# Joining the first attention's output projection with the normalisation behind it, and three changes of order around DMA queues

## The reference, cut to what matters

```python
n = layernorm(x)                                     # rows of 256
q, k, v = n @ Wq.T, ctx @ Wk.T, ctx @ Wv.T           # layer 0: 32 query heads of 8, 8 key groups
o = softmax(q k^T * 8**-0.5) v
x = x + o @ Wfc.T + bfc                              # the projection, its bias and the sum
x = x + moe_gelu(layernorm(x))                       # layer 0, feed-forward
...                                                  # layers 1 and 2
x = x + ffn_relu2(layernorm(x))                      # layer 2, feed-forward
x = x + attention_l3(layernorm(x), ctx)              # layer 3: 16 heads, keys quantised
x = x + moe_silu(layernorm(x))                       # layer 3: experts' weights are 16 x 512 KB of w1, 8 x 512 KB of w2
```

## Time and profile before

| | |
|---|---|
| median of 3 runs | 1090.81 us (1089.27 to 1090.97) |
| the profiled execution's own time | 1090.98 us |
| its span in the profile | 1089.3 us |
| first attention, first to last of its instructions | 16.2 to 177.7 us |
| its projection and normalisation, to the first instruction behind | 178.0 to 195.6 us |
| ffn_relu2's last DVE instruction, next block's first | 620.6 and 625.6 us |

### The profile page before, as it was taken

How to read it: one execution, slowest core, us unless ns; L and a number is a source line. 1 busy time by engine, 2 the same in 40 slices (tenths; PEclk the granted TensorE clock), 3 DMA queues, 4 the chain that set the end, 5 groups by cost and what they waited for, 6 DMA issues and landing times. The chain is left out here.

```text
span 1089.3 us, 15385 instructions
## 1 busy us (share of the span) xinstructions
PE 931.0 (85%) x5416; PEld 540.0 (50%) x5416; DVE 618.8 (57%) x1290; ACT 528.1 (48%) x797; POOL 257.7 (24%) x304
## 2 busy tenths in 40 slices
PE   5689897999799548889979678888888799999997
PEld 2244444666469415434436543343345565666664
DVE  4667764444534777725456489999995431211214
ACT  3166664322243584577843248899896211222210
POOL 4001010000000000414423236766775050000014
PEclk9689999899899869999979985555555699999999
DMA  3611410100358102576550647878653021111013
GB/s 116 168 34 53 112 37 12 38 1 1 116 60 69 32 0 78 149 181 141 81 202 23 143 150 146 166 131 193 143 101 67 0 78 44 49 44 44 25 34 101
DMA packets 130541, 91.63 MB, mean 84 GB/s; under 512 B 92853, under 2 KB 119775, under 8 KB 128687
## 3 DMA queue, kind: packets, MB, share of 16 engines
q1 hardware_dynamic: 125618, 83.45, 34.0%
q0 software_dynamic: 1536, 4.20, 1.2%
q10 hardware_dynamic: 3312, 3.02, 0.8%
HBM read 56.09 MB, written 15.86 MB: 66 GB/s over the span
## 5 line engine op out<-in xcount | busy, mean ns | idle before, releaser
L2360 ACT ACTIVATE sb_l_E<-PS,sb_l_NB,sb_L3SQS 128x1024 uint8<-128x1024 f32 x128 | 154.5, 1207 | 18.7 <-DVE sb_l_NB L2409 9.2
L2406 DVE TENSOR_REDUCE sb_l_NM<-PS 128x1 f32<-128x1024 f32 x128 | 155.5, 1215 | 1.9 <-PE PS L2307 1.9
L2307 PE MATMUL PS<-sb_l_K,sb_l_Q 128*128 128x512 bf16 x256 | 127.2, 599 | 30.4 <-ACT sb_l_E L2360 19.9
L2251 POOL CAST sb_l_ET<-sb_l_EP 128x1024 bf16<-128x1024 uint8 x127 | 128.1, 1046 | 57.1 <-DMA sb_l_EP<-sb_l_E 52.9
L613 DVE TENSOR_REDUCE sb_negmax<-PS 128x2 f32<-128x512 f32 x128 | 84.1, 690 | 32.0 <-PE PS L463 31.7
L2317 PEld LDWEIGHTS PS<-sb_L3VI,sb_l_ET 128*128 128x128 bf16 x1024 | 55.8, 113 | 68.3 <-issue 49.3
L599 ACT ACTIVATE sb_E<-PS 128x1024 f32<-128x1024 f32 x64 | 65.5, 1024 | 42.6 <-PE PS L526 42.5
L1368 PE MATMUL PS<-sb_L3w,sb_block_xT 128*128 x184 | 82.8, 593 | 0.7 <-issue 0.7
L923 ACT ACTIVATE sb_E<-PS 128x1024 f32<-128x1024 f32 x64 | 65.4, 1024 | 24.9 <-PE PS L830 21.2
L463 PE MATMUL PS<-sb_K,sb_Q 96*128 96x256 bf16 x256 | 54.0, 303 | 15.9 <-ACT sb_negmax_T L573 10.3
L846 POOL MEMSET sb_rms_eps<- 128x1 f32 x1 | 0.1, 100 | 275.5 <-POOLq L180 275.5
(11 more groups left out here) (356 smaller groups left out, 1768.3 us busy)
## 6 DMA issues: line engine op xcount, KB each, us to landing
sb_Q<-q SPq DMA_DIRECT2D x48, 192.0 KB
sb_L3w<-L3w SPq DMA_DIRECT2D x16, 512.0 KB, 7.1
sb_K<-k SPq DMA_DIRECT2D x24, 192.0 KB
sb_W2E<-L3w SPq DMA_DIRECT2D x8, 512.0 KB, 4.3
q<-sb_q_parts SPq DMA_DIRECT2D x12, 256.0 KB, 4.1
xs<-zero_row SPq DMA_DIRECT2D x1, 2944.0 KB, 47.2
sb_block_x<-xs SPq DMA_DIRECT2D x23, 128.0 KB, 2.1
ys<-sb_block_y ACTq DMA_DIRECT2D x23, 128.0 KB, 2.4
```

What stands on the lines that cost most here:

```text
L2251: return eng.tensor_copy(ET[:, u % CRING], EP[:, u // 2 % TRING, :, :, u % 2])
L2307: ins = pe.matmul(core.bank(2 * (n % SRING) + half), Q[:, h % RING, t * P:(t + 1) * P], K[:, h % RING, half * HALF:(half + 1) * HALF], sta ...
L2360: act.activation(E[:, n // 2 % ERING, :, n % 2], S(n), ACT.Exp, bias=NB[:, n:n + 1], scale=scale_of(h, t), accum_out=ZS[:, n:n + 1]).then_ ...
L2406: dve.tensor_reduce(NM[:, n:n + 1], S(n), axis=AX.X, op=ALU.max, negate=True).then_inc(maxed, 1)
```

## The change

- `project_norm` replaces `out_project` and the `layer_norm` behind it: one block, with the order of the last attention's end. The bias is added to tiles 0 to 3 by DVE at the start of its list and to tiles 4 to 7 by POOL; the bias itself is loaded during the attention as one of its prefetches.
- `attention_l0`: slot 0 of Q is written straight from the parts in SBUF, 9 DMAs of 64 KB (send_q), and the stores of the first half follow them. Groups 2 and 3 are loaded after the first and second copy of maxima. The first two copies of maxima are sent by ACT's own queue. The exp table is loaded before. copy_max stands ahead of the exp.
- `ffn_relu2`: the last six w1 loads go to the end of the list that `attention_l3` works off head by head (18 entries instead of 12), and the wait for the stores of k16 moves from the end of the block to just before attention_l3's key loads.

```diff
@@ -250,68 +251,137 @@
...
-def out_project(core, Wo, bias_dram):
...
+def project_norm(core, Wo, BB, weights):
     nc = core.nc
...
+    HN = NT // 2
+    old = core.take_old()
...
+    features = lambda half, c: core.XT[:, c, half * HALF:(half + 1) * HALF]
...
         with nc.Block() as block:
             @block.sync
             def _(sp):
...
+                sp.wait_ge(out_done, NT // 2)
+                for dst, src in weights:
+                    sp.dma_start(dst, src).then_inc(core.weights_in, 16)
+            @block.gpsimd
+            def _(pool):
+                for t in range(HN, NT):
+                    pool.tensor_tensor(core.X[:, t, :], core.X[:, t, :], BB[:, :], ALU.add).then_inc(biased_p, 1)
+                for handle in old:
+                    pool.sem_clear(handle)
             @block.tensor
             def _(pe):
                 for half in range(2):
                     for c in range(NC):
...
+                        for j in range(HN):
+                            ins = pe.transpose(core.PS[:, 2 * half + c, j * P:(j + 1) * P],
+                                               core.XN[:, HN * half + j, c * P:(c + 1) * P], core.identf[:, :])
+                        ins.then_inc(out_turned, 1)
+                for half in range(2):
+                    pe.wait_ge(xt_a, half + 1)
+                    pe.wait_ge(xt_v, half + 1)
+                    for t in range(HN * half, HN * half + HN):
+                        for c in range(NC):
+                            ins = pe.matmul(core.PS[:, 4 + t // 2, (t % 2) * D:(t % 2 + 1) * D],
+                                            core.XT[:, c, t * P:(t + 1) * P], Wo[:, c, :],
+                                            start=(c == 0), stop=(c == NC - 1))
+                        if t % 2:
+                            ins.then_inc(out_done, 1)
+                for half in range(2):
+                    for j in range(HN):
+                        t = HN * half + j
+                        pe.wait_ge(ln_a if t % 2 else ln_v, t // 2 + 1)
+                        for c in range(NC):
                             ins = pe.transpose(core.PS[:, 2 * half + c, j * P:(j + 1) * P],
                                                core.XN[:, t, c * P:(c + 1) * P], core.identf[:, :])
...
+                            if j == HN - 1:
+                                ins.then_inc(ln_turned, 1)
             @block.scalar
             def _(act):
                 act.preload_act_table_set("sqrt_and_others")
                 for half in range(2):
...
+                    act.wait_ge(out_turned, 2 * half + 1)
+                    act.activation(features(half, 0), core.bank(2 * half), ACT.Copy).then_inc(xt_a, 1)
+                for half in range(2):
+                    T = slice(HN * half, HN * half + HN)
+                    act.wait_ge(aggr, HN * (half + 1))
+                    act.activation(SD[:, T], MV[:, T, 1], ACT.Sqrt, bias=core.ln_eps[:, 0:1]).then_inc(std, 1)
+                    act.wait_ge(shift, half + 1)
+                    for t in range(HN * half + 1, HN * half + HN, 2):
+                        act.activation(core.XN[:, t, :], core.X[:, t, :], ACT.Identity, bias=SH[:, t:t + 1],
+                                       scale=RS[:, t:t + 1]).then_inc(ln_a, 1)
+                for half in range(2):
+                    act.wait_ge(ln_turned, 2 * half + 1)
+                    act.activation(features(half, 0), core.bank(2 * half), ACT.Copy)
             @block.vector
             def _(dve):
+                def add_out(pair):
+                    dve.wait_ge(out_done, pair + 1)
+                    dve.tensor_tensor(core.X[:, 2 * pair:2 * pair + 2, :],
+                                      core.PS[:, 4 + pair, :].rearrange("p (t d) -> p t d", d=D),
+                                      core.X[:, 2 * pair:2 * pair + 2, :], ALU.add).then_inc(added, 1)
+                def stats(pair):
+                    dve.wait_ge(added, pair + 1)
+                    for t in (2 * pair, 2 * pair + 1):
+                        core.row_stats(dve, t).then_inc(measured, 1)
+                def mean_var(half):
+                    dve.wait_ge(measured, HN * (half + 1))
+                    for t in range(HN * half, HN * half + HN):
+                        dve.bn_aggr(MV[:, t, :], core.ST[:, t, :]).then_inc(aggr, 1)
+                def normalise(half):
+                    T = slice(HN * half, HN * half + HN)
+                    dve.wait_ge(std, half + 1)
+                    dve.reciprocal(RS[:, T], SD[:, T]).then_inc(rstd, 1)
+                    dve.wait_ge(rstd, half + 1)
+                    dve.scalar_tensor_tensor(out=SH[:, T], in0=MV[:, T, 0], scalar=-1.0, in1=RS[:, T],
+                                             op0=ALU.mult, op1=ALU.mult).then_inc(shift, 1)
+                    for t in range(HN * half, HN * half + HN, 2):
+                        dve.tensor_scalar(core.XN[:, t, :], core.X[:, t, :], MV[:, t, 0:1], RS[:, t:t + 1],
+                                          ALU.subtract, ALU.mult).then_inc(ln_v, 1)
+                for t in range(HN):
+                    dve.tensor_tensor(core.X[:, t, :], core.X[:, t, :], BB[:, :], ALU.add).then_inc(biased_v, 1)
                 for half in range(2):
...
+                    dve.wait_ge(out_turned, 2 * half + 2)
+                    dve.tensor_copy(features(half, 1), core.bank(2 * half + 1)).then_inc(xt_v, 1)
+                dve.wait_ge(biased_v, HN)
+                add_out(0)
+                add_out(1)
+                stats(0)
+                stats(1)
+                mean_var(0)
+                dve.wait_ge(biased_p, HN)
+                add_out(2)
+                normalise(0)
+                add_out(3)
+                stats(2)
+                stats(3)
+                mean_var(1)
+                normalise(1)
+                for half in range(2):
+                    dve.wait_ge(ln_turned, 2 * half + 2)
+                    dve.tensor_copy(features(half, 1), core.bank(2 * half + 1))
...
 def attention_l0(core, Wq, Wk, Wv, VE, q8, k8, ones_dram, scale, prefetch):
@@ -408,6 +478,9 @@
                         load_k(g, r)
                         load_q(g, r)
 
+                def send_q(i, r):
+                    sp.dma_start(Q[PR * r + i:PR * (r + 1):PARTS, 0, :], QP[0:R8 * PER, 0, i, :]).then_inc(q_in[0], 16)
+
                 def load_max(n):
                     g, h = n // 2, n % 2
                     sp.wait_ge(max_out, n + 1)
@@ -422,19 +495,22 @@
                 sp.wait_ge(padded, 1 + RING)
                 sp.dma_start(K[RK:RK + PARTS, :, :].rearrange("p r t -> p (r t)"), ones_dram).then_inc(k_ones, 16)
                 for i, done in enumerate((high, middle, low)):
-                    store_q(0, i, done, stored_q0)
                     sp.wait_ge(stored_k[i], 16)
                     load_k(0, i)
-                sp.wait_ge(stored_q0, 16 * PARTS)
-                for r in range(PARTS):
-                    load_q(0, r)
+                    sp.wait_ge(done, 4)
+                    for r in range(PARTS):
+                        send_q(i, r)
+                for i, done in enumerate((high, middle, low)):
+                    store_q(0, i, done, stored_q0)
                 for i, done in enumerate((high, middle, low)):
                     store_q(1, i, done, stored_q1)
+                sp.wait_ge(stored_q0, 16 * PARTS)
                 load(1)
-                load(2)
-                load(3)
+                for g in range(2, RING):
+                    sp.wait_ge(max_out, g - 1)
+                    load(g)
                 sp.wait_ge(stored_q1, 16 * PARTS)
-                for n in range(HALVES):
+                for n in range(2, HALVES):
                     load_max(n)
                     g = n // 2
                     if n % 2 and g >= 1:
@@ -455,7 +531,7 @@
                 def max_scores(m):
                     g, b, j = m // MAXES, m % MAXES // PER, m % PER
                     if m % MAXES == 0:
-                        pe.wait_ge(q_in[g % RING], 16 * PARTS * (g // RING + 1))
+                        pe.wait_ge(q_in[g % RING], 16 * PARTS * (g // RING + (PARTS if g % RING == 0 else 1)))
                         pe.wait_ge(k_in[g % RING], 16 * PARTS * (g // RING + 1))
                     wait_shared(("max", m))
                     for i in range(2):
@@ -573,6 +649,14 @@
                     act.activation(MT[:, h, :], core.bank_bf16(shared_bank(("turn_max", n)))[0:PARTS * PER, 0:HALF],
                                    ACT.Copy).then_inc(max_out, 1)
 
+                def send_max(n):
+                    g, h = n // 2, n % 2
+                    act.wait_ge(max_out, n + 1)
+                    for i in range(PARTS):
+                        q = Q[RK + i:RK + i + 1, g % RING, :].rearrange("p (j t) -> p j t", t=TOK)
+                        act.dma_start(q[:, :, h * HALF:(h + 1) * HALF], MT[PER * i:PER * (i + 1), h, :]
```

(33 more changed lines are left out.)

55 lines of the change are left out of this document (15 added, 40 removed).

## The result

| | before | after |
|---|---|---|
| median of 4 runs each, same chip | 1090.47 us (1089.27 to 1090.97) | 1077.56 us (1073.85 to 1081.93) |
| ratio, 95% interval | | 0.9885 (0.9842 to 0.9928) |
| the profiled execution's own time, span | 1090.98, 1089.3 us | 1081.93, 1080.2 us |

The change gains 12.9 us, where 20.1 were forecast: 1077.56 against 1071, and 0.06 us outside the stated range of 1065.5 to 1077.5. The profiled execution of after is the slowest of its four.

The account below looks back on a forecast made before the run. PE was taken as the bound, busy 85% of the span, so gains lay where it idles. Terms 10.2 + 6.5 + 4.75 - 1.3 = 20.1 us, from 1090.98 to 1071 us; range 1065.5 to 1077.5.

Parts of the forecast that it names:

- The start of the attention: First attention's start: earlier first scores and no wait before step 0, 6.5 us gained in all (3 to 7).
- 9 sends of 0.5 to 0.6 ... the issues end at 33.3 to 34.0: SP's sends of Q's slot 0 in the first attention: Q there at 35.4, gain 2.2 us (0.1 to 2.6).
- The 4.61 us wait goes: PE's wait before the first attention's step 0, for the maxima written to Q, vanishes; step 0 starts at 48.4.
- 3 DMAs of 0.5 us: ACT's issues of the first maxima in the first attention, after its copy; they were to cost nothing.
- "Cost 0" behind ffn_relu2: After ffn_relu2's 4.75 us gain, the moved k16 wait and six loads cost 0 (loads 0 to 1).
- The joined block: First projection with normalisation: gain 1.5 us without contention, but DVE's and POOL's adds cost 2.8; net cost 1.3.
- The copy ahead of the exp: First attention's steps: PE's 0.79 us wait for ACT's copy of maxima goes 13 times, 10.2 us gained (7 to 10.3).
- Rival B: First attention's steps: DVE or the exp becomes the bound, half the 0.79 us waits return, 1076 us; chance 0.10.
- Rival D: First attention: maxima rows still behind SP's group loads (n = 4, 6, 8, 10) land late, 1091 us and more; chance 0.03.
- "Against it": The argument against rival D: the trace of before shows no PE wait for the rows of maxima after step 0.
- Rival C: First attention's start: group 1 late or maxima behind group 2, 2 to 3.5 us less gain, 1073.5 us; chance 0.14.
- a PE clock that falls one stretch earlier: PE's clock falling or rising one stretch earlier, with the terms' bounds, gives the forecast's own range, 1068 to 1074 us.

Follow-up runs that it names:

- f3_split_sends: The changed kernel with the nine sends of Q's slot 0 shared, six issued by SP and three by ACT: 1072.28 us, ratio 0.9837 to the kernel before.
- f1_adds_later: The changed kernel with DVE's four bias adds behind its two copies in the joined block: 1073.26 us, ratio 0.9842 to the kernel before.
- c_after: The changed kernel unaltered, traced and timed again on another chip: 1076.13 us, ratio 0.9872 to the kernel before.
- g2_both: The changed kernel with DVE's bias adds behind its copies and the nine sends shared by SP and ACT: 1071.73 us, ratio 0.9788 to the kernel before.
- g4_both_longer: The changed kernel with both amendments (later bias adds, shared sends) and 40 more ACT instructions: 1071.20 us, ratio 0.9818 to the kernel before.
- f4_loads_after: The changed kernel with SP's loads of groups 2 and 3 issued only once the preceding rows of maxima have landed: 1078.93 us, ratio 0.9898.
- g1_longer_list: The changed kernel with 40 more one-column copies in ACT's list before the first maxima: 1076.61 us, ratio 0.9849 to the kernel before.
- c_before: The kernel before unaltered, for a second trace: 1093.83 us, ratio 0.9993 to the kernel before beside it.
- e4_start_only: The kernel before with only the change's edit of the first attention's start (sends, load order, maxima by ACT, exp table): 1088.68 us, ratio 0.9959.

## Why the prediction was wrong

The traces together give each term with less chance in it. Mean durations in us between matmuls, over the traces that have the part as it was, as changed, and amended (number of traces; the change leaves the other stages alone):

| stage | as before | changed | amended | forecast gain | gain in the traces |
|---|---|---|---|---|---|
| first matmul of attention to step 0 | 40.1 (5) | 35.8 (5) | 32.4 (3), f3 | 6.5 | 4.3 |
| step 0 to the attention's end | 121.8 (5) | 110.8 (9) | | 10.2 | 11.0 |
| projection and normalisation | 17.5 (5) | 19.2 (6) | 15.6 (3), f1 | -1.3 | -1.7 |
| moe_gelu | 81.3 (5) | 83.0 (6) | 82.6 (3), f1 | 0 | -1.8 |
| ffn_relu2's last matmul to the next stage's first | 8.6 (5) | 4.1 (9) | | 4.75 | 4.5 |
| normalisation and projections of attention_l3 | 13.9 (5) | 15.7 (9) | | 0 | -1.8 |
| sum | | | | 20.1 | 14.5 |

14.5 stands beside 12.9 and, for c_after, 13.9 in time. The column "amended" holds f1_adds_later or f3_split_sends, g2_both and g4_both_longer.

- *The start of the attention* is the step that failed first: "9 sends of 0.5 to 0.6 ... the issues end at 33.3 to 34.0". They take 0.67 to 0.74 us each, and 0.5 to 0.6 is what the earlier trace rows have for a 32 KB write of another shape. For the first scores 2.2 us were forecast; over the traces, counted from the attention's first matmul, they come 0.3 us earlier (21.9 and 21.6). The lower bound of 0.1 us was right, the value 2.2 wrong. And "The 4.61 us wait goes" held only in part: a wait of 1.77 us is left. "3 DMAs of 0.5 us" by ACT were 1.48, 0.59 and 0.58. The prediction had cited the Trainium skill (DMA: Bandwidth & Descriptors, Queues, rings and completion order) for ACT's rows not queueing behind SP's group. They didn't queue for the whole group: counted from the first of the three issues they took 6.6 us, against 9.1 in the earlier trace rows, and from the end of the third 3.9, against 7.2. But being served in turn was not free either: 1.1 us by the latter count without the group beside them (f4_loads_after).
- *"Cost 0" behind ffn_relu2* was right for the k16 wait, for attention_l3's heads and for the last transpose, and wrong for PE: in all nine traces in which the pause ahead of it is gone, normalisation and projections of attention_l3 take 15.5 to 16.0 us, and 13.9 to 14.0 in the five that have the pause. It is the clock: over the 32 matmuls 0.77 to 0.81 is granted in the nine, and 1.00 in the five. 1.8 of 4.5 us went back.
- *The joined block* was right in mechanism: the adds lock each other out and the copy stands behind them (first copy expected at 182, in the old count, that is 4.2 us into the block; it came at 3.5). DVE's adds took 3.6 us, not the 4.2 that were charged, and where PE kept its clock (g1_longer_list) the block cost 0.5 us, not 1.3. What was missing is PE's clock behind the longer gap, 8.83 us for 7.15, which the text named as a bound and did not charge.
- *moe_gelu* starts at half clock (0.50 to 0.52 over its first 10 us, 0.66 in the other three) in all nine traces with a joined block, and in two of the five without (c_before, e4_start_only). That the block makes it likelier fits, but isn't shown.
- *The copy ahead of the exp* was right and a little low: 11.0 for 10.2. Rival B fell: neither DVE nor the exp became a bound. Rival D fell as a forecast of the time, but its mechanism is there at one of its four places, n = 10: in all nine traces with the copy ahead PE waits 0.4 to 1.7 us for the rows of maxima at step 40, 1.1 in the mean. In after SP issued them from 114.36 on, and PE was held until 121.25. "Against it" rested on the trace of before, which has no such wait; three of the five traces with the copy behind have one of 0.4 to 1.3 us, which is 0.5 in the mean of the five. Rival C, the start gains less, was true; it had 0.14 and 1073.5 us, and alone would not have explained the time either.
- The range named a PE clock that falls one stretch earlier, but gave it no size of its own. The two stages behind, moe_gelu and the start of attention_l3, in which nothing was changed, took 3.6 us more, and the sum has 0 for both. For moe_gelu's half of it the cause stays open.
- That the time lies only 0.06 us outside the range says little for the mechanism: the steps gained 0.8 us more than forecast, which hid part of the loss.

## What to carry to other kernels

Count a DMA's issue from a row of the same shape, and when several of them stand ahead of the critical load, share them over two issuing engines. Put an operation whose inputs are both in SBUF behind the PSUM copy that another engine waits for, whenever POOL works on SBUF beside it. A pause that is taken away ahead of TensorE may come back in part as half clock: charge it, and read stages from several traces, since one execution can be 5 us off in a place that nobody touched.

## What was not expected of the hardware

- In moe_silu's end ACT is held for 3.8 to 4.7 us beyond its producer, in 13 of 14 traces, of unlike kernels, while POOL issues its 16 gathers; the stage takes 3 to 5 us more with it. The profile names no steady cause ("remote" or a DMA), and the cause is open.
- The kernel before, on other chips, ran from 1086 to 1100 us, where four runs on the first one lay within 1.7 us. With 5 to 12 runs of a kernel the 95% intervals there reach 2.6 to 4.4 us to either side.
